# Stacking on two queues, sums and fillers on TensorE: a transformer block of self-attention, cross-attention and MLP

## The chip, the cores and the metric

The kernel runs on one NeuronCore of a Trainium2 chip. The metric is the device time of one execution in microseconds (us), the median of three runs. The engines are TensorE (PE for its matmuls, PEld for its weight loads), VectorE (DVE), ScalarE (ACT), GpSimd (POOL) and SyncE (SP, which only issues DMAs here).

## The reference

One block over x of 2 x 2048 tokens and 512 features, 16 heads of 32, with 154 context tokens per batch, in fp32:

```
xn = layer_norm(x, ln0);  q, k, v = heads(xn @ qkv_w.T)
x = x + merge(softmax(q k^T * scale) v) @ sa_proj_w.T          # self-attention
xn = layer_norm(x, ln1);  q = heads(xn @ q_w.T); k, v from the context
x = x + merge(softmax(q k^T * scale + mask) v) @ ca_proj_w.T   # cross-attention
xn = layer_norm(x, ln2)
x = x + (gelu(xn @ fc1_w.T + fc1_b) @ fc2_w.T + fc2_b)
```

## The kernel before

The program is six phases, one after the other, with a barrier of all engines between two of them: `qkv` (0 to about 311 us of the profile), `self` (to 2016), `context` (to 2066), `cross` (to 2651), `late` (to 2809) and `mlp`. Each fp32 product is split into a high and a low part (fp32r), so that three matmuls stand for one. All synchronisation is written out by hand: each engine has its own list of instructions in program order, and semaphores tie the lists. There is no scheduler. What stands behind a waiting instruction on its engine waits too.

**Self-attention** (`self_phase`) has 32 stages of 512 queries x 4 heads x 2048 keys. In a stage TensorE makes 64 first passes (scores for the row maximum, L1529, those of the stages ahead), 64 second passes (scores less maximum, L1559), and 16 times four small matmuls that weigh v with the exponentials (L1572). VectorE takes the maxima (L1697), ScalarE the exponentials (L1647). For the softmax's denominators GpSimd adds the 16 key tiles of exponentials in 8 pairs, p0 to p7 (`add_pair`, L1470), into four buffers `part_sum`, and adds one buffer onto another by accumulating DMAs of 1 MB (`add_half`, L1475): after p2, p3, p4, p5 and p6, five in a stage. At the end of block 1 of the next stage (there are 8 blocks in a stage) TensorE adds up over the partitions with ones (`add_up`, L1592) in three groups of 8 matmul instructions: one part waits for the last DMA into it, the second for p7, the third for the DMA that carries p6. Which buffer has which role changes from stage to stage (`sum_parts`), and p0 of a stage waits for the previous stage's last DMA.

**Cross-attention** (`cross_phase`) has 8 tiles of 512 tokens, 0 to 7, and 4 groups of 4 heads in each. For tile t: `project` (the output projection of self-attention, added to x, 48 matmuls), layer norm on VectorE with a power on GpSimd, `turn` (transposes), `result` (the query product, four groups of 12 matmuls into a ring `dense` of two PSUM banks, which project, turn and the maxima use too), `high_result` and `low_result` (ScalarE and VectorE split each group's result into `r_high` and `r_low`, two buffers each), `stack_q` (SP copies the parts into `q`, three places for each of four heads: 12 DMAs a group, 48 a tile), `first_pass` (L811), the maxima (`maxima`, L1100; `turn_max`; `split_max`; `send_max`, ScalarE's two DMAs into `q`), `second_pass` (L828), `exponential` (L977), `weigh_both` (L840), `add_pair` on GpSimd and `add_up` on TensorE (L850), `invert` (four reciprocals, L1117) and `divide` (L1124). `period(t)` weaves the second passes of tile t with the transposes, results and first passes of tile t+1 and the projection of tile t+2. Ahead of `period(0)` the first tile is prepared in series: project(0), norm, turn(0), the bias of the query product (L932), result(0), project(1), then the first passes of groups 0 and 1. In tile 7 nothing is left to weave in.

## Time and profile before

| | us |
|---|---|
| median of three runs | 3553.53 (3552.98 to 3554.64) |
| the profiled execution, its own time | 3546.62 |
| its span in the profile | 3544.8 |
| self-attention, 324 (first matmul) to 2016 | 1692 |
| cross-attention, 2066 to 2651 | 585 |

The profile is one execution. A windows row gives the busy time of each engine in a stretch with the number of its instructions, the mean granted clock of TensorE (1.00 is 2.4 GHz, 0.50 is 1.2 GHz) and the DMA engines' share. A timeline row gives start, length, engine, line, operation, what is written from what, shapes, how many instructions were merged, and in brackets how long the engine sat idle before and what ended it. SPq and ACTq are DMA issues.

### The profile page before, as it was taken

To read this page: it belongs to the slowest core of one execution; us is meant where nothing else is said; L and a number is where in the kernel's file an instruction comes from. 1 tells how busy PE (TensorE), PEld (TensorE's weight loads), DVE (VectorE), ACT (ScalarE), POOL (GpSimd) and SP (SyncE) were. 2 spreads that over 40 slices of the span, in tenths; PEclk is the share of its full clock that TensorE was granted. 3 is DMA by queue.
4 is the path that set the end of the run, shared out by engine and by line. 5 is a ranking of instruction groups with operands and counts; after the bars stand their busy time and mean duration, and the time that the engine had idled before them with its cause. 6 is when DMAs were issued, how large, how long until landed. Compare 5 with 4: busy or idle time off the path is not lost. (4 is left out here: it accounts for less than half of the span.)

```text
span 3544.8 us, 43782 instructions
## 1 busy us (share of the span) xinstructions
PE 3272.3 (92%) x16448; PEld 2124.6 (60%) x16448; DVE 2075.4 (59%) x3643; ACT 1541.8 (43%) x2826; POOL 1602.5 (45%) x531
## 2 busy tenths in 40 slices
PE   7998999999999999999999668898978599999999
PEld 5885555555555555555555245666536488888887
DVE  4444887778777877777787035777647532222222
ACT  2321566666666666666566413343424321111111
POOL 0001678888887888888788622343421000000000
PEclk9997899999999999999999778999959799999999
DMA  4446277677667766776675553433328721111110
GB/s 171 176 170 181 60 169 153 133 155 156 153 136 163 154 142 140 166 152 141 147 153 116 117 147 105 129 113 116 103 68 286 267 90 45 45 45 47 48 48 24
DMA packets 200516, 454.44 MB, mean 128 GB/s; under 512 B 34114, under 2 KB 57224, under 8 KB 176752
## 3 DMA queue, kind: packets, MB, share of 16 engines
q1 hardware_dynamic: 173167, 282.80, 26.0%
q0 software_dynamic: 23040, 167.78, 23.5%
q8 instruction: 130, 2.13, 0.2%
q10 hardware_dynamic: 4096, 1.06, 0.2%
q14 instruction: 83, 0.67, 0.1%
HBM read 154.47 MB, written 102.82 MB: 73 GB/s over the span
## 5 line engine op out<-in xcount | busy, mean ns | idle before, releaser
L1697 DVE TENSOR_REDUCE self_part_max<-self_first 128x1 f32<-128x512 f32 x2048 | 1250.4, 678 | 352.2 <-PE self_first L1529 352.0
L1470 POOL TENSOR_TENSOR self_part_sum<-self_expo 128x2048 f32<-128x2048 f32 x256 | 1187.5, 4647 | 274.1 <-DMA self_part_sum<-self_part_sum 209.2
L1647 ACT ACTIVATE self_expo<-self_second 128x512 f32<-128x512 f32 x2048 | 1039.3, 622 | 482.6 <-PE self_second L1559 471.5
L1529 PE MATMUL self_first<-self_k,self_q 96*128 96x512 f32 x2048 | 854.9, 425 | 13.0 <-DMA self_k<-k_t 13.0
L1559 PE MATMUL self_second<-self_q,self_k 98*128 98x512 f32 x2048 | 828.1, 406 | 14.9 <-DVE self_max_low L1709 7.0
L1529 PEld LDWEIGHTS self_first<-self_k,self_q 96*128 96x128 f32 x2048 | 397.9, 194 | 301.2 <-DVE self_part_max L1697 162.4
L1559 PEld LDWEIGHTS self_second<-self_q,self_k 98*128 98x128 f32 x2048 | 386.9, 189 | 187.0 <-ACT self_expo L1647 53.2
L1572 PE MATMUL self_weighted<-self_expo,self_v_sb 128*32 128x512 f32 x4096 | 498.3, 605 | 0.0
L2037 DVE CAST mlp_h_high<-mlp_h 128x512 fp32r<-128x512 f32 x128 | 54.8, 428 | 507.0 <-PE mlp_out_sum L61 507.0
L2012 ACT ACTIVATE mlp_h<-mlp_hidden_sum,mlp_b_col 128x512 f32<-128x512 f32 x128 | 88.3, 690 | 603.2 <-PE mlp_hidden_sum L61 603.2
L1572 PEld LDWEIGHTS self_weighted<-self_expo,self_v_sb 128*32 128x32 f32 x4096 | 107.7, 109 | 231.9 <-ACT self_expo L1647 121.0
L977 ACT ACTIVATE cross_expo<-cross_second 77x512 f32<-77x512 f32 x256 | 145.1, 592 | 216.0 <-PE cross_second L828 211.8
L726 POOL TENSOR_TENSOR cross_pair_sum<-cross_expo 77x2048 f32<-77x2048 f32 x32 | 146.2, 4569 | 178.5 <-ACT cross_expo L977 178.5
L59 PE MATMUL mlp_hidden_sum<-mlp_xt_high,mlp_w_high 128*128 128x512 f32 x512 | 203.2, 397 | 24.1 <-DMA mlp_xt_low<-xn_t 24.1
L60 PE MATMUL mlp_hidden_sum<-mlp_xt_low,mlp_w_high 128*128 128x512 f32 x512 | 202.7, 396 | 0.0
L60 PE MATMUL mlp_out_sum<-mlp_w_low,mlp_h_high 128*128 128x512 f32 x512 | 202.4, 395 | 0.0
L61 PE MATMUL mlp_out_sum<-mlp_w_high,mlp_h_low 128*128 128x512 f32 x512 | 202.2, 395 | 0.0
L61 PE MATMUL mlp_hidden_sum<-mlp_xt_high,mlp_w_low 128*128 128x512 f32 x512 | 201.9, 394 | 0.0
L59 PE MATMUL mlp_out_sum<-mlp_w_high,mlp_h_high 128*128 128x512 f32 x512 | 201.9, 394 | 0.0
L1100 DVE TENSOR_REDUCE cross_row_max<-cross_first 128x2 f32<-128x308 f32 x256 | 113.5, 454 | 87.7 <-PE cross_first L811 87.6
L1475 POOL DMA_DIRECT2D self_part_sum<-self_part_sum x160 | 141.3, 883 | 50.4 <-POOL self_part_sum L1470 37.5
L811 PEld LDWEIGHTS cross_first<-cross_k,cross_q 98*128 98x128 f32 x512 | 107.4, 224 | 50.2 <-DVE cross_row_max L1100 24.9
(162 smaller groups left out, 3848.0 us busy)
## 6 DMA issues: line engine op xcount, KB each, us to landing
self_part_sum<-self_part_sum POOLq DMA_DIRECT2D x160, 1024.0 KB, 8.3
self_k<-k_t SPq DMA_DIRECT2D x96, 256.0 KB, 9.0
self_q<-q_t SPq DMA_DIRECT2D x93, 256.0 KB, 4.7
cross_q<-cross_r_high SPq DMA_DIRECT2D x256, 64.0 KB, 2.0
qkv_x<-in_x SPq DMA_DIRECT2D x8, 1024.0 KB, 6.5
v<-qkv_v_sb SPq DMA_DIRECT2D x32, 256.0 KB, 2.1
q_t<-qkv_r_high SPq DMA_DIRECT2D x32, 256.0 KB, 2.0
q_t<-qkv_r_low SPq DMA_DIRECT2D x32, 256.0 KB, 2.3
```

What stands on the lines that cost most here:

```text
L59: nc.tensor.matmul(out, left_high, right_high, start=first, stop=False)
L60: nc.tensor.matmul(out, left_high, right_low, start=False, stop=False)
L61: return nc.tensor.matmul(out, left_low, right_high, start=False, stop=last)
L726: nc.gpsimd.tensor_tensor(pair_sum[0:width, g % pair_slots], expo[0:width, u], expo[0:width, u + 1], ALU.add).then_inc(pair_done, 1)
L977: nc.scalar.activation(expo[0:width, unit % e_slots, a], second[0:width, at % s_ring], ACT.Exp, scale=scale).then_inc(exp_done, 1)
L1470: nc.gpsimd.tensor_tensor(to, expo[:, t % p_slots], expo[:, (t + 1) % p_slots], ALU.add).then_inc(pair_done, 1)
L1475: pool.dma_start(part_sum[:, half].rearrange("p a t -> p (a t)"), part_sum[:, part].rearrange("p a t -> p (a t)"), accum_op=ALU.add).then_inc(
L1529: nc.tensor.matmul(first[:, n % f_ring], q[0:base, c % q_slots, a, s * P:(s + 1) * P], k[0:base, c // stages_per_group % 2, a, k0:k0 + TOK ...
L1559: nc.tensor.matmul(second[:, s_slot[n]], k[0:exp_rows, c // stages_per_group % 2, a, t * P:(t + 1) * P], q[0:exp_rows, c % q_slots, a], st ...
L1572: mm = nc.tensor.matmul(weighted[cols], v_sb[:, t, cols], expo[:, t % p_slots, a], start=t == 0, stop=t == n_k - 1)
L1647: nc.scalar.activation(expo[:, t % p_slots, a], second[:, s_slot[n]], ACT.Exp, scale=scale).then_inc(exp_done, 1)
L1697: nc.vector.tensor_reduce(part_max[:, a * SUB + s, k:k + 1], first[:, n % f_ring], AX_X, ALU.max).then_inc(first_read, 1)
```

## The change

Line numbers of the new kernel differ; the names are the same.

Self-attention: `add_up` has four groups instead of three. Groups 0 and 1 take the two buffers into which DMAs accumulate, groups 2 and 3 the sums p6 and p7 as GpSimd leaves them. So the DMA of p6 is gone (four a stage), the buffers keep their roles, and p0 to p3 of a stage wait for the groups 0 to 3 of the previous stage's `add_up`.

Cross-attention, start: the memset of `q` on GpSimd moves behind the first low part (`low_attn(0)`). The bias matmuls move ahead of the transposes, followed by 12 filler matmuls (`keep_busy`: a product of w_high that nobody reads). The results of groups 2 and 3 of tile 0 use the two idle `pair_sum` buffers, so that four groups have buffers of their own. ScalarE issues the DMAs of the low parts (16), SP the others (32). project(1) is woven with the first passes of group 0, and VectorE's and GpSimd's lists follow.

Cross-attention, end: fillers stand beside the first passes of group 1 of tile 7. `last_period` replaces `period(7)`: fillers, `add_last` (TensorE sums the exponentials itself, 16 matmul instructions in place of GpSimd's pair and 8), VectorE's finishing moved behind the last maxima, and a spare PSUM bank for the last sums.

```diff
+        def parts(t, g):
+            if t == 0 and g >= r_slots:
+                return r_spare[g - r_slots][:, 0], r_spare[g - r_slots][:, 1]
+            return r_high[:, g % r_slots], r_low[:, g % r_slots]
+
+        def stack(eng, t, g, places):
+            ge(eng, r_ready, groups * t + g + 1)
+            for j in places:
+                src = parts(t, g)[j % 2]
+                for a in range(heads):
+                    eng.dma_start(q[j * HEAD_DIM:(j + 1) * HEAD_DIM, heads * g + a].bitcast(F32),
+                                  src[a * HEAD_DIM:(a + 1) * HEAD_DIM].bitcast(F32)).then_inc(q_loaded[g], 16)
+
...
+                    if n < pair_slots:
+                        pool.wait_ge(q_loaded[r_slots + n], 16 * 3 * heads)
...
+                pool.wait_ge(rows_set, 1)
                 low_attn(0)
+                pool.wait_ge(a_ready, 1)
+                nc.gpsimd.memset(q[base:base + 4].bitcast(F32), 1.0).then_inc(rows_set, 1)
+                pool.wait_ge(rows_set, 2)
                 inverse_root(0)
...
+                def add_last(g):
+                    n = groups * last + g
+                    to = total if g < groups - 1 else dense[:, d_place[("maximum", last, 3)] % d_ring]
+                    if g < groups - 1:
+                        pe.wait_ge(mean_done, n)
+                    else:
+                        pe.wait_ge(max_split, n + 1)
+                    pe.wait_ge(exp_done, n_seconds * last + per_group * (g + 1))
+                    for kt in range(n_k):
+                        for a in range(heads):
+                            rows = slice(a * HEAD_DIM, (a + 1) * HEAD_DIM)
+                            mm = nc.tensor.matmul(to[rows], ones[0:width], expo[0:width, (n_k * g + kt) % e_slots, a],
+                                                  start=kt == 0, stop=kt == n_k - 1)
+                    mm.then_inc(total_done, 1)
...
+                def last_period():
+                    spare = dense_free(("maximum", last, 3))
+                    for n in range(per_group):
+                        second_pass(last, 0, n)
+                        first_pass(last, 2, n)
+                        keep_busy(spare, 1)
+                        if n == 5:
+                            add_up(last - 1, 3)
+                    for n in range(per_group):
+                        second_pass(last, 1, n)
+                        first_pass(last, 3, n)
+                        if n == 1:
+                            turn_max(last, 2)
+                        if n == 2:
+                            weigh_both(last, 0)
+                        if n == 5:
+                            add_last(0)
+                        keep_busy(spare, 1)
+                    spare = dense[:, d_place[("maximum", last, 2)] % d_ring]
+                    pe.wait_ge(max_split, groups * last + 3)
+                    for g in (2, 3):
+                        for n in range(per_group):
+                            second_pass(last, g, n)
+                            if n == 1 and g == 2:
+                                turn_max(last, 3)
+                            if n == 2:
+                                weigh_both(last, g - 1)
+                            if n == 5:
+                                add_last(g - 1)
+                            if n >= 2:
+                                keep_busy(spare, 2)
+                    weigh_both(last, 3)
+                    add_last(3)
...
+                    spare = None if has_after else dense_free(("maximum", t + 1, 1))
                     for n in range(items):
                         if has_next:
                             first_pass(t + 1, 1, n)
                         some(works[n // 4], 3)
+                        if not has_after:
+                            keep_busy(spare, 2)
...
                     rest(project(0, s))
-                for c in range(chunks):
-                    turn(0, c)
-                pe.wait_ge(w_ready, 2)
+                pe.wait_ge(w_loaded[1], 16)
                 pe.wait_ge(ln_loaded, 32)
                 for g in range(groups):
                     for c in range(chunks):
                         mm = nc.tensor.matmul(total[:, g:g + 1], w_raw[1][:, c, g * P:(g + 1) * P], shift[:, c:c + 1],
                                               start=c == 0, stop=c == chunks - 1)
                 mm.then_inc(bias_done, 1)
+                keep_busy(first[:, 0], 12)
+                for c in range(chunks):
+                    turn(0, c)
                 for g in range(groups):
                     rest(result(0, g))
-                for s in range(SUB):
-                    rest(project(1, s))
                 pe.wait_ge(ones_done, 1)
-                for g in range(2):
-                    for n in range(items):
-                        first_pass(0, g, n)
-                    turn_max(0, g)
-                for t in range(tiles):
+                for n in range(items):
+                    work = work if n % 2 else project(1, n // 2)
+                    some(work, 6)
+                    first_pass(0, 0, n)
+                    if n % 2:
+                        rest(work)
+                turn_max(0, 0)
+                for n in range(items):
+                    first_pass(0, 1, n)
+                    keep_busy(second[:, n % s_ring], 1)
+                turn_max(0, 1)
+                for t in range(last):
                     period(t)
-                add_up(tiles - 1, groups - 1)
+                last_period()
...
-                    ge(act, q_loaded[last % groups], 16 * 3 * heads * (t + 1 if last >= 0 else t))
-                    nc.scalar.activation(r_high[:, g % r_slots], dense[:, n % d_ring], ACT.Identity,
+                    if t == 1 and g < r_slots:
+                        act.wait_ge(q_loaded[g], 16 * 3 * heads)
+                    elif t > 0:
+                        before = g - r_slots
+                        act.wait_ge(q_loaded[before % groups], 16 * 3 * heads * (t + 1 if before >= 0 else t))
+                    nc.scalar.activation(parts(t, g)[0], dense[:, n % d_ring], ACT.Identity,
...
+                act.wait_ge(bias_ready, 1)
+                high_result(0, 0)
+                high_result(0, 1)
                 high_attn(1)
-                act.wait_ge(bias_ready, 1)
-                for g in range(groups):
-                    high_result(0, g)
+                high_result(0, 2)
+                stack(act, 0, 0, (1,))
+                high_result(0, 3)
+                stack(act, 0, 1, (1,))
+                stack(act, 0, 2, (1,))
+                stack(act, 0, 3, (1,))
...
+                        if n >= items - 2:
+                            invert(last - 1, 3, n - items + 2)
+                    for n in range(items):
+                        maxima(last, 3, n)
+                        if n == 0:
+                            split_max(last, 2)
+                        if n in (1, 2):
+                            invert(last - 1, 3, n + 1)
+                        if n == 2:
+                            divide(last - 1, 3)
+                    split_max(last, 3)
+                    for g in range(groups):
+                        finish(last, g)
...
+                for n in range(items):
+                    maxima(0, 0, n)
+                    if n % 2:
+                        add_projection(1, n // 2)
+                        stats_of(1, n // 2)
+                split_max(0, 0)
                 for s in range(SUB):
                     moments_of(1, s)
                 var_of(1)
-                for s in range(SUB):
-                    norm(1, s)
-                for g in range(2):
-                    for n in range(items):
-                        maxima(0, g, n)
-                    split_max(0, g)
-                for t in range(tiles):
+                for n in range(items):
+                    maxima(0, 1, n)
+                    if n >= SUB:
+                        norm(1, n - SUB)
+                split_max(0, 1)
...
-                def add_pairs(i, c):
-                    h0, h1, p0, p1 = sum_parts(c)
-                    ge(pool, half_added[0], 48 * i)
...
-                    ge(pool, total_done, n_sums * i)
-                    add_pair(i, 2, part_sum[:, p0])
-                    add_half(i, 2, 0, h0, p0)
-                    add_pair(i, 3, part_sum[:, p1])
...
+                def add_pairs(i):
+                    for p in range(4):
+                        ge(pool, total_done, n_sums * (i - 1) + p + 1)
+                        add_pair(i, p, part_sum[:, p])
+                        if p >= 2:
+                            add_half(i, p, p - 2, p)
                     if not (isinstance(i, int) and i == 0):
                         divide(i - 1)
-                    ge(pool, half_added[0], 48 * i + 16)
-                    add_pair(i, 4, part_sum[:, p0])
-                    add_half(i, 4, 0, h0, p0)
-                    ge(pool, half_added[1], 32 * i + 16)
...
+                    for p in range(4, n_pairs):
+                        half, part = p % 2, 2 + p % 2
+                        ge(pool, half_added[half], 32 * i + 16 * (p // 2 - 1))
+                        add_pair(i, p, part_sum[:, part])
+                        if p < n_pairs - 2:
+                            add_half(i, p, half, part)
...
-                    for n, part in enumerate((h1, p1, h0)):
-                        if n == 0:
-                            ge(pe, half_added[1], 32 * (i + 1))
-                        elif n == 1:
-                            ge(pe, pair_done, n_pairs * (i + 1))
+                    for n in range(n_sums):
+                        if n < 2:
+                            ge(pe, half_added[n], 32 * (i + 1))
                         else:
-                            ge(pe, half_added[0], 48 * (i + 1))
+                            ge(pe, pair_done, n_pairs * i + n_pairs - n_sums + n + 1)
```

On GpSimd in self-attention, one stage (L1470 is a pair's sum, L1475 an accumulating DMA, L1482 the division for the previous stage). Before:

```order
L1470 TENSOR_TENSOR self_part_sum<-self_expo 128x2048 x4
L1475 DMA self_part_sum<-self_part_sum 128x2048
L1470 TENSOR_TENSOR self_part_sum<-self_expo 128x2048
L1475 DMA self_part_sum<-self_part_sum 128x2048
L1482 TENSOR_TENSOR self_mean<-self_inverse,self_mean 128x512
L1470 TENSOR_TENSOR self_part_sum<-self_expo 128x2048
L1475 DMA self_part_sum<-self_part_sum 128x2048
L1470 TENSOR_TENSOR self_part_sum<-self_expo 128x2048
L1475 DMA self_part_sum<-self_part_sum 128x2048
L1470 TENSOR_TENSOR self_part_sum<-self_expo 128x2048
L1475 DMA self_part_sum<-self_part_sum 128x2048
L1470 TENSOR_TENSOR self_part_sum<-self_expo 128x2048 x4
```

The same stage now:

```order
L1575 TENSOR_TENSOR self_part_sum<-self_expo 128x2048 x5
L1580 DMA self_part_sum<-self_part_sum 128x2048
L1575 TENSOR_TENSOR self_part_sum<-self_expo 128x2048
L1580 DMA self_part_sum<-self_part_sum 128x2048
L1587 TENSOR_TENSOR self_mean<-self_inverse,self_mean 128x512
L1575 TENSOR_TENSOR self_part_sum<-self_expo 128x2048
L1580 DMA self_part_sum<-self_part_sum 128x2048
L1575 TENSOR_TENSOR self_part_sum<-self_expo 128x2048
L1580 DMA self_part_sum<-self_part_sum 128x2048
L1575 TENSOR_TENSOR self_part_sum<-self_expo 128x2048 x5
```

The DMA between p6 and p7 is gone; p6, p7 and the next stage's p0, p1, p2 follow each other directly.

On ScalarE in the first tile of cross-attention, from the transposed tile (L959) to the first maxima (L989). Before:

```order
L959 ACTIVATE cross_xt_high<-cross_dense 128x512 x4
L953 ACTIVATE cross_a_high<-cross_a_raw 128x2048
L966 ACTIVATE cross_r_high<-cross_dense,cross_q_bias 128x512 x4
L989 DMA cross_q<-cross_max_high 1x16x128
L989 DMA cross_q<-cross_max_low 1x16x128
```

And now:

```order
L1033 ACTIVATE cross_xt_high<-cross_dense 128x512 x4
L1043 ACTIVATE cross_r_high<-cross_dense,cross_q_bias 128x512 x2
L1027 ACTIVATE cross_a_high<-cross_a_raw 128x2048
L1043 ACTIVATE cross_pair_sum<-cross_dense,cross_q_bias 128x512
L637 DMA cross_q<-cross_r_low 32x512 x4
L1043 ACTIVATE cross_pair_sum<-cross_dense,cross_q_bias 128x512
L637 DMA cross_q<-cross_r_low 32x512 x4
L637 DMA cross_q<-cross_pair_sum 32x512 x8
L1067 DMA cross_q<-cross_max_high 1x16x128
L1067 DMA cross_q<-cross_max_low 1x16x128
```

Sixteen DMA issues have come onto ScalarE, and the copy of tile 1's attention (L953, now L1027) stands behind two results.

On TensorE at the end of tile 7, groups 2 and 3 (L828 second passes, L840 weighing, L850 sums). Before:

```order
L828 MATMUL cross_second<-cross_q,cross_k 77x512 x8
L840 MATMUL cross_weighted<-cross_expo,cross_v_sb 32x512 x8
L850 MATMUL cross_total<-cross_pair_sum,cross_ones 32x512 x4
L828 MATMUL cross_second<-cross_q,cross_k 77x512 x5
L840 MATMUL cross_weighted<-cross_expo,cross_v_sb 32x512 x8
L850 MATMUL cross_total<-cross_pair_sum,cross_ones 32x512 x8
```

And now, group 3 alone (L868 are fillers, L893 `add_last`):

```order
L868 MATMUL cross_dense<-cross_w_high 128x512 x2
L840 MATMUL cross_second<-cross_q,cross_k 77x512
L868 MATMUL cross_dense<-cross_w_high 128x512 x2
L840 MATMUL cross_second<-cross_q,cross_k 77x512
L893 MATMUL cross_total<-cross_expo,cross_ones 32x512 x8
L868 MATMUL cross_dense<-cross_w_high 128x512 x2
L840 MATMUL cross_second<-cross_q,cross_k 77x512
L868 MATMUL cross_dense<-cross_w_high 128x512 x2
L840 MATMUL cross_second<-cross_q,cross_k 77x512
L868 MATMUL cross_dense<-cross_w_high 128x512 x2
L852 MATMUL cross_weighted<-cross_expo,cross_v_sb 32x512 x8
L893 MATMUL cross_dense<-cross_expo,cross_ones 32x512 x8
```

The sums read the exponentials themselves, and fillers stand between the second passes.

## Rows read from the trace of the kernel before

**Rows 1.** Waits, self-attention (450 to 1950 us): who for whom, us, times, longest.
```profile
POOL self_part_sum L1470 <- DMA self_part_sum<-self_part_sum: 202.2, 106, 5.7
...
PEld self_second L1592 <- POOL self_part_sum L1470: 29.7, 17, 3.8
PEld self_second L1592 <- DMA self_part_sum<-self_part_sum: 23.7, 20, 3.1
```

**Rows 2.** Timeline, PE, line 1592: start, us, instruction, count, [idle before].
```profile
431.42 2.76 PE L1592 MATMUL self_second<-self_part_sum,self_ones 128*32 128x512 f32 x24
...
993.47 2.76 PE L1592 MATMUL self_second<-self_part_sum,self_ones 128*32 128x512 f32 x24
...
1043.47 1.90 PE L1592 MATMUL self_second<-self_part_sum,self_ones 128*32 128x512 f32 x16
...
1967.43 2.75 PE L1592 MATMUL self_second<-self_part_sum,self_ones 128*32 128x512 f32 x24
...
2009.74 1.04 PE L1592 MATMUL self_second<-self_part_sum,self_ones 128*32 128x512 f32 x8
2013.58 2.89 PE L1592 MATMUL self_second<-self_part_sum,self_ones 128*32 128x512 f32 x16 [2.80 <-POOL self_part_sum L1470]
```

**Rows 3.** Timeline, POOL: two self-attention stages, first three sums and last.
```profile
1046.07 13.68 POOL L1470 TENSOR_TENSOR self_part_sum<-self_expo 128x2048 f32<-128x2048 f32 x3 [1.87 <-DMA self_part_sum<-self_part_sum]
...
1091.10 4.56 POOL L1470 TENSOR_TENSOR self_part_sum<-self_expo 128x2048 f32<-128x2048 f32 x1 [0.71 <-DMA self_part_sum<-self_part_sum]
...
1300.97 13.69 POOL L1470 TENSOR_TENSOR self_part_sum<-self_expo 128x2048 f32<-128x2048 f32 x3 [1.17 <-DMA self_part_sum<-self_part_sum]
...
1348.66 4.51 POOL L1470 TENSOR_TENSOR self_part_sum<-self_expo 128x2048 f32<-128x2048 f32 x1 [0.27 <-DMA self_part_sum<-self_part_sum]
```

**Rows 4.** Timeline, ACT, POOL and DVE, start of cross-attention.
```profile
2074.28 1.91 ACT L953 ACTIVATE cross_a_high<-cross_a_raw 128x2048 fp32r<-128x2048 f32 x1 [22.56 <-DMA cross_a_raw<-self_t]
...
2071.20 6.92 POOL L711 MEMSET cross_q<- 4x8192 f32 x1
2078.21 6.47 POOL L716 TENSOR_TENSOR cross_a_low<-cross_a_raw,cross_a_high 128x2048 fp32r<-128x2048 f32 x1
...
2117.19 4.58 POOL L716 TENSOR_TENSOR cross_a_low<-cross_a_raw,cross_a_high 128x2048 fp32r<-128x2048 f32 x1 [15.04 <-ACT cross_a_high L953]
...
2078.02 2.29 DVE L1193 TENSOR_TENSOR cross_w_low<-cross_expo,cross_w_high 128x2048 fp32r<-128x2048 f32 x1 [11.68 <-ACT cross_w_high L1034]
```

**Rows 5.** Timeline, PE, first tile of cross-attention.
```profile
2084.78 0.76 PE L766 MATMUL cross_dense<-cross_w_high,cross_a_high 128*128 128x512 f32 x1 [22.41 <-POOL cross_a_low L716]
...
2105.12 1.97 PE L780 MATMUL cross_dense<-cross_identity,cross_a_raw 128*128 128x128 f32 x8 [6.46 <-DVE cross_a_raw L1079]
...
2109.42 6.83 PE L932 MATMUL cross_total<-cross_shift,cross_expo 128*128 128x1 f32 x32
2116.11 0.77 PE L792 MATMUL cross_dense<-cross_xt_high,cross_w_high 128*128 128x512 f32 x1
```

**Rows 6.** Timeline (SP, ACT) and windows while the first tile is stacked.
```profile
2122.97 2.44 SPq L651 DMA_DIRECT2D cross_q<-cross_r_high  x4
...
2139.57 0.69 ACT L966 ACTIVATE cross_r_high<-cross_dense,cross_q_bias 128x512 fp32r<-128x512 f32 x1 [6.90 <-DMA cross_q<-cross_r_high]
...
2122.89:2153.30 30.41, 22.04 (x82) 16.77 (x80) 8.17 (x18) 2.06 (x3) 0.00 (x0) 0.89 0.40 99
2144.85:2151.15 6.30, 6.30 (x29) 5.06 (x27) 2.77 (x4) 0.00 (x0) 0.00 (x0) 1.00 0.42 104
2151.15:2166.98 15.83, 8.64 (x35) 7.05 (x34) 11.31 (x30) 0.00 (x0) 1.01 (x1) 0.62 0.27 88
```

**Rows 7.** Window and timeline (PE, DVE), last tile of cross-attention.
```profile
2590.70:2598.70 8.00, 7.98 (x31) 6.87 (x31) 4.86 (x11) 5.31 (x10) 0.94 (x1) 0.50 0.02 4
...
2599.83 3.64 PE L840 MATMUL cross_weighted<-cross_expo,cross_v_sb 77*32 77x512 f32 x16
...
2644.20 3.40 DVE L1117 RECIPROCAL cross_total<-cross_total 128x128 f32<-128x128 f32 x4 [2.06 <-PE cross_total L850]
```

75 lines of the change are left out of this document (30 added, 45 removed).

## The prediction

> **What bounds the kernel now.** The phases run one after the other, so gains in different phases add up. I read self-attention by its waits first. GpSimd waits 202 us in 106 pieces for its own accumulating DMAs, and TensorE's weight loads wait 29.7 and 23.7 us in the sums over the partitions, for GpSimd's last pair and for the last DMA [rows 1]. TensorE is otherwise always at work, so these waits lengthen the phase. How much they cost is read from the timeline of TensorE's sums [rows 2]. Where a sum runs through in one piece (24 instructions, 2.76 us, at 993.47), the next one starts 50.00 us later. From the first (431.42) to the one at 1967.43 there are 30 periods in 1536.0 us, 36.0 more than 30 x 50.00. The last period, with no more first passes, is 42.31 us. So a stage is 50.0 us of TensorE, and 36 us are waits.
>
> In cross-attention the tiles in the middle are woven tightly; the first and the last are not. In the first, TensorE begins after 22.41 us of waiting for GpSimd's low part [rows 5], the bias (6.83 us) stands between the transposes and the results [rows 5], and then all hangs on stacking: from 2122.97 SP issues 4 DMAs in 2.44 us, 0.63 each, 48 in 30.4 us [rows 6]. ScalarE's fourth result waits 6.90 us for a buffer that such a DMA reads [rows 6], and TensorE's projection of tile 1, its ring of two banks and everything behind it wait for that result. In the last tile TensorE's granted clock is 0.50, that is 1.2 GHz. 31 matmuls, about ten pairs of second and first passes, take 8.00 us there [rows 7].
>
> **Self-attention.** A group of 8 matmul instructions adds (2.76 - 1.04) / 2 = 0.86 us, from a sum in one piece and one cut off after its first group [rows 2]. It stands on TensorE's path: 31 x 0.86 = 26.7 us more. What goes is the wait. The DMA of p6 is no longer waited for by anyone. p7 now has three groups ahead of it, 2.6 us, where it had one. And GpSimd gets ahead: it sheds a DMA issue (0.9 us between p6 and p7) and the wait ahead of its next p0, 1.87 and 1.17 us in the two stages shown [rows 3]. Its own chain from p0 to the end of p7 takes 49.6 us (1046.07 to 1095.66) and 52.2 in one of the slowest stages (1300.97 to 1353.17) [rows 3]. The new wait is that p0 needs TensorE's group 0, 0.9 us after the sum begins. With that start and 52.2 us, p7 ends at 0.9 + 52.2 - 50.86 = 2.2 us into the next sum, still ahead of its group at 2.6; with 49.6 it ends before the sum begins. So I take all 36.0 us as gone; if one wait in ten survives it is 4 us. At the phase's end one group instead of two follows p7 (1.04 of the 2.89 us [rows 2]): 1.8 less. Sum: 26.7 - 36.0 - 1.8 = **-11.1 us**, with -12 and -3 as ends.
>
> **First tile, up to the first stacked result.** The memset of q (6.92 us) leaves GpSimd's path, and the low part of tile 0 starts when ScalarE's copy ends (2076.2) instead of 2078.21 [rows 4]. It took 6.47 us where the same operation takes 4.58 at 2117.19 [rows 4]. VectorE's low weights ran from 2078.02 to 2080.31, and 2080.31 + 4.4 is when GpSimd ended: the one that came second stood still. Now GpSimd comes first, ends at 2080.8, and VectorE's 2.29 us, which the projection needs as well, end at 2083.1 rather than 2080.31. TensorE starts at 2083.1: -1.7.
>
> The Trainium skill, page "SBUF — State Buffer", says of the port pair that VectorE and GpSimd share that "issue order, not op shape, decides who blocks". By that rule the start is 2083.1; by a plain sharing of the slowdown it would be 2082.7, 0.4 us better. The rows agree with the rule.
>
> The bias now fills the wait for the normalization. It and the 12 fillers take 3.4 + 2.8 us at 2.4 GHz and 6.8 + 5.1 at 1.2; starting at 2097.0 (2084.78 + 13.9 for 48 matmuls, less 1.7) they end between 2103.2 and 2108.9, and the normalized tile is there at 2103.4 (2105.12 - 1.7) [rows 5]. I take 2104, nearer to the fast end, since TensorE comes out of 48 dense matmuls. Results follow the transposes after 4.5 us, at 2108.5 instead of 2116.11 [rows 5]: -7.6 so far. The first result's 12 matmuls run at 1.2 GHz in the profile; a warmer start gives 0 to 2.4 us, I take 1.2. The first stacking DMA goes out at 2114.2, not 2122.97: **-8.8**.
>
> **First tile, from there to the first second pass.** Before it is 2166.98 - 2122.97 = 44.0 us: stacking and project(1) to 2151.15, then 15.8 us of first passes [rows 6]. Call the first DMA's start S. With four buffers the results no longer wait for DMAs: all four groups are ready at S + 8.8. ScalarE copies tile 1's attention at S + 2.0 (it now stands behind two results, 1.9 us), GpSimd's low part (4.58 us [rows 4]) ends at S + 8.6, and project(1) starts there. Group 0 is stacked at S + 9.3 (SP's eight issues end at S + 5.1, ScalarE's four at S + 7.3, 2 us to land). Then 48 matmuls at 0.233 us (6.30 us for 27 [rows 6]) and 8 first passes at 0.37 make 14.2 us, to S + 22.8. What remains of the 15.8 us is group 1 with the statistics and normalization of tile 1 between its maxima: 8.5 us. Second passes start at S + 31.3: **-12.7 us**. All that hides is the stacking of groups 1 to 3 (SP until S + 20.2, ScalarE until S + 15.6), wanted from S + 23 on.
>
> The Trainium skill, page "DMA: Bandwidth & Descriptors", section "Issuing engines are not separate DMA queues", has two queues share the same 16 DMA engines, so that the second saves only the time of issuing. Here issuing is what takes the time: the engines' share is 0.40 while one queue issues without a pause [rows 6]. The sum changes by neither: with SP alone group 1 would be stacked by S + 17, still ahead of its use. I expect the gain from the buffers and the weave, and from the second queue next to nothing.
>
> **Last tile.** Before: 2590.70 to the end of the last division, 2644.20 + 3.40 + 0.69 = 2648.3, 57.6 us [rows 7]. Now, at 2.4 GHz: 0.9 us for the new wait on the split maximum of group 1 (its PSUM bank is the fillers'). Group 0: 8 x (second 0.23 + first 0.19 + filler 0.23) + 0.86 = 6.1. Group 1: the same 5.2, weighing 1.7 (half of 3.64 [rows 7]), `add_last` 1.7, some 1.0 for VectorE: 9.6. Groups 2 and 3: 8 second passes, 12 fillers, 1.7 + 1.7, each 8.6, and 1.0 once for a division that `add_last(1)` waits for. Then weighing and the last sum 3.4, reciprocals and division 4.1 [rows 7]. That is 42.4; with 1.4 for handoffs 43.8: **-13.8 us**. The fillers themselves are 28 x 0.23 = 6.4 us on the path, which pay only if the clock stays at 2.4 GHz. The eight pairs of fillers in tile 6 lie beside maxima that VectorE paces. The GpSimd pair that goes (4.5 us) was beside TensorE, not on the path, except at the end.
>
> **The sum.** 11.1 + 8.8 + 12.7 + 13.8 = 46.4 us. The profiled execution took 3546.6 us (span 3544.8) and would take 3500.2. The median of the runs is 3553.5, 6.9 more than the profiled one; I see no row for that and carry it over: 3553.5 - 46.4 = **3507**.
>
> **Rivals.** (1) *GpSimd's chain paces self-attention after all.* For: GpSimd waits 202 us for DMAs that stay [rows 1], and p0 is now tied to TensorE's sum. Against: 49.6 us against 50.86. If half of the waits stay, 18 us are lost: 3525. (2) *The clock stays at 1.2 GHz in the last tile.* For: it is so now, and has not risen although TensorE was busy 7.98 of 8.00 us [rows 7]. Against: the tile before leaves TensorE busier than it was when the clock fell, and the fillers are matmuls like those from 2144.85 on, whose clock is 1.00 [rows 6]. Then the 40.2 us of TensorE and waits before the last 3.4 + 4.1 grow by about 27 in all, the tile takes 71 us, and the kernel 3534. (3) *Something in the first tile takes the place of the buffer wait*, the normalization of tile 1 or the copy on ScalarE behind the results: half of the 21.5 us comes, 3518. (4) *Slower than before:* the loop from group 0 to p0 to p7 becomes the stage's length. Each stage has four DMAs in series with eight sums; if they landed so much later that the chain took over 50.86 + 46.4 / 31 = 52.4 us in every stage, the rest's gain would be eaten. At 53.0 it is 31 x 2.1 = 66 us more in self-attention: 3573. The slow stage shown, 52.2, is close, but few stages come near it, and there is a DMA less. (5) *The change does not do what it says*: the fillers or the queue turn out inert; that lies within the range.
>
> **How the numbers follow.** Forecast 0.68 (3499 to 3516); rival 1 0.09, rival 2 0.09, rival 3 0.10, rival 4 0.03, and 0.01 for a result within 0.2% of before, about what a measurement of this kernel can tell from no change. The range of 8 in 10 takes in rivals 1 and 3 in part and stops short of 2: 3497 to 3527. Faster by over 0.2%: 0.96; within: 0.01; slower: 0.03.
>
> **What would show it.** In the profile of the changed kernel the sums of self-attention should stand 50.9 us apart throughout, 32 instructions in one piece, with no wait for GpSimd or a DMA. In cross-attention TensorE should start about 17 us after the barrier, the second passes of tile 0 about 21 us earlier than before from the phase's start, and the last tile should have a granted clock of 1.00 and take 44 us. The prediction is wrong if self-attention's sums still wait, if that clock is 0.50, or if TensorE waits more than 2 us for a normalization in the first tile.

## The result, and the profile after

The changed kernel takes 3499.84 us (median; 3498.54 to 3504.63), the kernel before 3553.53: 53.7 us less. The ratio, 0.9863 with an interval of 0.9845 to 0.988, gives a little less than the medians: 49 us (43 to 55). The forecast was 3507, 46.4 us less. The profiled execution of the changed kernel is its slowest, 3504.63 us (span 3502.8), 42.0 us shorter than the profiled one of before.

By phase, between the barriers, in the two profiled executions and in a second one of the kernel before that an experiment below gave:

| us | before | before, second profile | after |
|---|---|---|---|
| start of the program to cross-attention's barrier | 2066.2 | 2073.4 | 2058.6 |
| cross-attention: barrier to the first second pass | 100.8 | 100.8 | 77.3 |
| tiles 0 to 6, to the first second pass of tile 7 | 423.7 | 423.4 | 424.1 |
| tile 7, to the end of the last division | 57.6 | 57.9 | 44.2 |
| what follows, to the end of the span | 896.5 | 898.2 | 898.7 |

**Self-attention.** The timeline of TensorE's sums, which stands against [rows 2]: in the stages shown a sum is one piece of 32 instructions with no wait in front. In 30 of the 32 stages it takes 3.6 us so; the other two sums take 3.85 and 4.01.

```profile
430.84 3.62 PE L1682 MATMUL self_second<-self_part_sum,self_ones 128*32 128x512 f32 x32
...
991.20 3.62 PE L1682 MATMUL self_second<-self_part_sum,self_ones 128*32 128x512 f32 x32
...
1042.06 3.62 PE L1682 MATMUL self_second<-self_part_sum,self_ones 128*32 128x512 f32 x32
...
2006.40 3.65 PE L1682 MATMUL self_second<-self_part_sum,self_ones 128*32 128x512 f32 x32
```

The waits of the same phase (who for whom, us, times, longest), against [rows 1]:

```profile
POOL self_part_sum L1575 <- DMA self_part_sum<-self_part_sum: 190.1, 91, 5.9
...
POOL self_part_sum L1575 <- PE self_second L1682: 43.2, 23, 4.7
...
PEld self_second L1682 <- POOL self_part_sum L1575: 3.2, 7, 1.1
```

GpSimd still waits for its DMAs, 190 us instead of 202, and has a new wait of 43 us for TensorE's sums; but TensorE's weight loads wait 3.2 us where they waited 29.7 + 23.7. GpSimd's timeline, against [rows 3], shows the two ends of that loop: p7 ends at 1037.22 + 4.59 = 1041.81, just ahead of the sums (1042.06), and p0 starts 1.2 us behind their first instruction; from there to the next p7's end (1093.62) it is 50.4 us.

```profile
1037.22 4.59 POOL L1575 TENSOR_TENSOR self_part_sum<-self_expo 128x2048 f32<-128x2048 f32 x1 [1.51 <-DMA self_part_sum<-self_part_sum]
1043.22 13.70 POOL L1575 TENSOR_TENSOR self_part_sum<-self_expo 128x2048 f32<-128x2048 f32 x3 [1.40 <-PE self_second L1682]
...
1089.04 4.58 POOL L1575 TENSOR_TENSOR self_part_sum<-self_expo 128x2048 f32<-128x2048 f32 x1 [1.55 <-DMA self_part_sum<-self_part_sum]
```

**First tile.** The barrier is at 2058.56 here and was at 2066.18. Timeline of GpSimd, VectorE, TensorE and SP, against [rows 4] and [rows 5]:

```profile
2069.02 4.50 POOL L722 TENSOR_TENSOR cross_a_low<-cross_a_raw,cross_a_high 128x2048 fp32r<-128x2048 f32 x1 [5.50 <-ACT cross_a_high L1027]
...
2070.70 4.97 DVE L1299 TENSOR_TENSOR cross_w_low<-cross_expo,cross_w_high 128x2048 fp32r<-128x2048 f32 x1 [11.98 <-ACT cross_w_high L1112]
...
2075.82 0.77 PE L778 MATMUL cross_dense<-cross_w_high,cross_a_high 128*128 128x512 f32 x1 [21.08 <-DVE cross_w_low L1299]
...
2088.76 3.63 PE L998 MATMUL cross_total<-cross_shift,cross_expo 128*128 128x1 f32 x32
2092.26 4.60 PE L868 MATMUL cross_first<-cross_w_high 128*128 128x512 f32 x12
2096.69 1.03 PE L792 MATMUL cross_dense<-cross_identity,cross_a_raw 128*128 128x128 f32 x8
...
2105.44 10.24 SPq L637 DMA_DIRECT2D cross_q<-cross_r_high  x16
```

The bias takes 3.63 us and not 6.83. TensorE's first second pass is at 2135.89. The window from the first stacking DMA to it (busy time of PE, PEld, DVE, ACT, POOL with counts, clock, DMA share, GB/s), against [rows 6]:

```profile
2105.44:2135.89 30.45, 26.55 (x120) 21.27 (x119) 16.82 (x39) 3.87 (x4) 5.60 (x2) 0.91 0.58 163
```

**Last tile.** Windows, against [rows 7] (the second is a stretch of an ordinary tile, for later), and the last reciprocals and division:

```profile
2564.00:2598.70 34.70, 34.02 (x214) 15.96 (x216) 22.05 (x36) 17.58 (x32) 0.00 (x0) 1.00 0.07 25
...
2257.00:2263.80 6.80, 5.95 (x25) 5.58 (x26) 4.49 (x10) 3.37 (x7) 0.00 (x0) 0.50 0.04 12
...
2600.01 3.40 DVE L1206 RECIPROCAL cross_dense<-cross_dense 128x128 f32<-128x128 f32 x4 [1.51 <-PE cross_dense L893]
2603.45 0.69 DVE L1213 TENSOR_TENSOR cross_mean<-cross_dense,cross_mean 128x512 f32<-128x512 f32 x1
```

The clock is 1.00 as long as TensorE works on the tile, where it was 0.50.

### The profile page after: what moved, and what is told of

Read it like the earlier page. It is cut to its first block and busy times, and to the rows that moved or that the text cites. A ratio compares the mean times of both kernels' runs of the same rounds, so it can differ in the third digit from the quotient of the medians.

```text
span 3502.8 us, 44500 instructions
## 1 busy us (share of the span) xinstructions
PE 3281.3 (94%) x16812; PEld 2133.4 (61%) x16812; DVE 2078.2 (59%) x3643; ACT 1541.9 (44%) x2826; POOL 1553.9 (44%) x495
## 5 line engine op out<-in xcount | busy, mean ns | idle before, releaser
L734 POOL TENSOR_TENSOR cross_pair_sum<-cross_expo 77x2048 f32<-77x2048 f32 x28 | 128.1, 4574 | 133.9 <-ACT cross_expo L1055 133.9
L1580 POOL DMA_DIRECT2D self_part_sum<-self_part_sum x128 | 112.9, 882 | 41.0 <-POOL self_part_sum L1575 33.1
```

Source lines behind the costliest of these rows:

```text
L734: nc.gpsimd.tensor_tensor(pair_sum[0:width, g % pair_slots], expo[0:width, u], expo[0:width, u + 1], ALU.add).then_inc(pair_done, 1)
```

## The experiments

All ratios are to the kernel before on the same chip. The times of one kernel scatter by 9 to 25 us on the chips of the experiments, more than in the first measurement. The changed kernel itself was timed only in the first measurement, so an experiment is held against it by the two ratios, which are good to some 6 to 8 us each. Where a single stretch is in question, the profile decides it; each kernel has one.

### One part at a time

Three kernels hold one part each; a fourth is the kernel before, unchanged, with a second profile.

```diff
# x1_self: only (cut)
-    n_sums = 3
+    n_sums = 4
# with the loops on GpSimd and TensorE that follow from it
```

> The kernel before with the change of self-attention alone (four groups of sums, the DMA of p6 gone). Theory A, the prediction's: eight more matmul instructions a stage cost 26.7 us and all 36.0 us of waits go, so the whole is about 11 us faster than before (between 3 and 12). Theory B: the profile of the changed kernel shows only 7.6 us gained ahead of cross-attention, since one stage took 54.2 us and the clock was low at the phase's end; if that is the rule and not one execution's accident, the gain is 7 to 8 us. Theory C: GpSimd's chain or the DMAs still pace some stages in most executions, gain under 4 us. If the parts add up, this one is also what is left of 53.7 us when the first tile (about 23) and the last (about 13) are taken off: 17 us, and then the profiled execution of before flatters before.

Measured: 3541.84 us, ratio 0.9976 (0.9962 to 0.9989), 8.5 us less by the ratio (4 to 13). In its profile the barrier of cross-attention stands at 2058.8, 14.6 us ahead of the second profile of before. Its cross-attention, which is that of before, is 5.1 us longer than in that profile (590.5 us against 585.4): two tiles took 64.9 us, where that profile has one and the first none, and tile 6 took 60.8 instead of 57.5. So in the phase itself the gain is above theory A's, theory C falls, and the time alone would have misled.

`x2_first` has only what changed at the start of cross-attention, as in the diff of the change: the memset behind the low part, the bias and 12 fillers ahead of the transposes, four buffers, `stack` on SP and ScalarE, the weave with 8 fillers.

> The kernel before with the changes at the start of cross-attention alone (memset behind the low part, bias ahead of the transposes with 12 fillers, four result buffers, two stacking queues, project(1) woven with first passes). Theory A: the parts are independent, and it gains what the two profiles show between the barrier and the first second pass, 100.8 - 77.3 = 23.5 us (the prediction had 21.5). Theory B: a later phase gives some of it back (the granted clock of the tiles behind it, or the period in which the second passes start at 1.2 GHz), gain 15 to 20 us.

Measured: 3526.64 us, ratio 0.9928 (0.9905 to 0.995), 26 us less (18 to 34). In the profile 77.2 us from the barrier to the first second pass, and cross-attention 560.3 us, 25.1 less. Theory A.

```diff
# x3_last: only (cut; add_last, the fillers and VectorE's new order come with it)
-    for t in range(tiles): period(t)
+    for t in range(last): period(t)
+    last_period()
```

> The kernel before with the changes at the end of cross-attention alone (fillers in tile 6 and 7, sums on TensorE, the finishing behind the last maxima). Theory A: 13 to 14 us faster, last tile 44 us at a granted clock of 1.00 throughout. Theory B: whether the clock holds hangs on how the tile before was met, and in a kernel with another start it falls in some executions: then 3 to 8 us, with a clock of 0.50 for part of the tile and times that scatter.

Measured: 3538.69 us, ratio 0.9968 (0.9951 to 0.9984), 11 us less (6 to 17). Last tile 44.2 us in the profile. Theory A. The three sum up to 8.5 + 25.6 + 11.4 = 45.5 us by their ratios and to 15 + 25 + 12 = 52 us by their profiles; the whole change is 49 us by its ratio and 54 by the medians. Within that scatter the parts add up.

> The kernel before once more, unchanged, for its profile beside its times. The prediction carried over 6.9 us between the profiled execution (3546.6) and the median (3553.5) with no row for it. Theory A: it is chance of one execution or another chip, and a second profile shows a time within 2 us of the median, with more waiting in self-attention than the 36 us read from the first one. Theory B: profiled executions are always shorter than timed ones by about 7 us; then this profile is again near 3546.

Measured: 3555.38 us, ratio 1.0003 (0.9985 to 1.0021), profiled span 3553.7 us. Theory A: profiled executions are not short as such. The timeline of its sums, start, length, instruction, count and wait:

```profile
431.19 2.76 PE L1592 MATMUL self_second<-self_part_sum,self_ones 128*32 128x512 f32 x24
...
2016.99 1.04 PE L1592 MATMUL self_second<-self_part_sum,self_ones 128*32 128x512 f32 x8
...
2020.79 2.92 PE L1592 MATMUL self_second<-self_part_sum,self_ones 128*32 128x512 f32 x16 [2.75 <-POOL self_part_sum L1470]
```

The last sum starts 1585.8 us behind the first, and 1578.3 in [rows 2]. The kernels x2 and x3, whose self-attention is that of before, have 1586.6 and 1585.8. An execution with 1578.3 is the odd one of four: beyond 30 periods of 50.00 us and a last one of 42.3 it has 36 us, which are the waits, the others 43.5 to 44.3. (It is also the only one of the four from the first measurement; whether the execution or the chip makes the difference is open.)

### The cushion of three groups

```diff
# y5_p7_first: the groups in the order p7, buffer 0, buffer 1, p6
-                    for n in range(n_sums):
+                    for at in range(n_sums):
+                        n = (at - 1) % n_sums
# and GpSimd's waits for the groups in the same order
-                        ge(pool, total_done, n_sums * (i - 1) + p + 1)
+                        ge(pool, total_done, n_sums * (i - 1) + (p + 1) % n_sums + 1)
```

> The changed kernel with the four groups of sums in self-attention in another order: p7 first, then the two buffers of the DMAs, then p6 (GpSimd's waits follow the same order). It tests the cushion: in the changed kernel p7 is read last, 2.6 us behind the start of the sums, and in its profiles GpSimd ends p7 between 7 us before the start and 3.5 us behind it. Theory A: those 2.6 us are what swallows the waits. Read first, p7 is late in 20 of the 31 stages by 0.2 to 3.5 us, some 26 us in all by the changed kernel's profile, less what GpSimd gains back from waiting less; the phase is 15 to 30 us longer and most of the gain over the kernel before is gone. Theory B: the missing DMA of p6 is what helped, and the order does not matter: under 5 us.

Measured: 3545.32 us, ratio 0.9976 (0.9961 to 0.9991). The barrier of cross-attention is at 2109.0 instead of 2058.6, 50 us later. But the profiled execution is this kernel's slowest, 3558.51 us, 13 above the median; by the two ratios the order costs some 40 us. Either way it is theory A's mechanism, above the 30 us that I gave it. Its sums and GpSimd's timeline:

```profile
1011.50 3.62 PE L1683 MATMUL self_second<-self_part_sum,self_ones 128*32 128x512 f32 x32
...
1062.98 3.64 PE L1683 MATMUL self_second<-self_part_sum,self_ones 128*32 128x512 f32 x32 [0.44 <-POOL self_part_sum L1575]
...
1013.51 13.69 POOL L1575 TENSOR_TENSOR self_part_sum<-self_expo 128x2048 f32<-128x2048 f32 x3 [3.00 <-PE self_second L1683]
...
1058.26 4.58 POOL L1575 TENSOR_TENSOR self_part_sum<-self_expo 128x2048 f32<-128x2048 f32 x1 [1.25 <-DMA self_part_sum<-self_part_sum]
1065.01 13.68 POOL L1575 TENSOR_TENSOR self_part_sum<-self_expo 128x2048 f32<-128x2048 f32 x3 [2.17 <-PE self_second L1683]
```

Now a loop closes: the sums wait for p7, GpSimd's next p0 waits 2.2 to 3.0 us for the first groups of the sums, and from p0 to the end of p7 it needs 49.3 us (1013.51 to 1062.84). The stage is what the loop takes, 51.5 us here and 52.3 on average ((2054.70 - 432.67) / 31), where TensorE has 50.9 of work. I had priced the delays one by one, as if GpSimd could recover; in a loop each is paid for by the next stage too. In the changed kernel the same loop is 50.4 + 1.2 us (the rows above) less the 2.6 of the groups ahead of p7, 49.0 against 50.9. With p7 first the whole gain in self-attention is lost, and more. What the missing DMA of p6 brings by itself was not tried.

### The first tile: queue, buffers, weave

```diff
# y1_one_queue
-                    stack(sp, t, g, (0, 1, 2) if t > 0 else (0, 2))
+                    stack(sp, t, g, (0, 1, 2))
-                stack(act, 0, 0, (1,))        # and those of groups 1 to 3
```

> The changed kernel with all 48 stacking DMAs of the first tile on SP, none on ScalarE. Theory A, the prediction's: the second queue is worth next to nothing. Group 0 is stacked after SP's twelve issues (7.6 us) instead of eight, about 2 us later, ahead of the projection's first part, whose GpSimd copy it waits for anyway; the first second pass starts within 1 us of 77.3 us behind the barrier, and the time is that of the changed kernel within 1 us. Theory B: issuing bounds the first tile, so the groups come 7.6 us apart and the second passes of tile 0 start 5 us or more later.

Measured: 3501.8 us, ratio 0.9865 (0.9849 to 0.9882); first second pass 77.2 us behind the barrier. Theory A.

```diff
# y3_two_buffers
-            if t == 0 and g >= r_slots:
-                return r_spare[g - r_slots][:, 0], r_spare[g - r_slots][:, 1]
# ScalarE stacks groups 0 and 1 ahead of results 2 and 3, which wait for them
```

> The changed kernel with two result buffers in the first tile as before (groups 2 and 3 wait until groups 0 and 1 are stacked), and all else changed: two queues, the weave, bias and fillers. Theory A: the buffers are a large part of the 12.7 us (13.5 measured) between the first stacking DMA and the first second pass. Group 2's result then waits for group 0's stacking, about 9 us behind the first DMA, group 3's for group 1's, about 14 us, and the projection of tile 1 with them: second passes 4 to 8 us later. Theory B: the weave hides the buffers' wait, as the maxima and the normalization of tile 1 set the end: under 2 us.

Measured: 3505.44 us, ratio 0.9878 (0.9859 to 0.9897); first second pass 78.3 us behind the barrier. Theory B, by the profile. (The profiled execution takes 3512.86 us, its slowest; two of its tiles take 66.2 and 65.7 us, where the changed kernel has one of 65.0.)

```diff
# y8_two_buf_one_q: both of these
```

> The changed kernel with two result buffers and one stacking queue in the first tile, as before; weave, bias, fillers and the rest as changed. One queue alone cost nothing (first second pass 77.2 us behind the barrier), two buffers alone 1.0 us (78.3). Theory A: either one hides the lack of the other, and both together cost more than the sum: the third result waits for twelve issues and a landing (9.6 us behind the first DMA), the fourth for twelve more (17.2), the projection's second part for that, and second passes start 4 to 7 us later. Theory B: the weave hides both, under 2 us.

Measured: 84.5 us to the first second pass, 7.2 later than in the changed kernel: a little over theory A's range. ScalarE's timeline shows the wait of [rows 6] back, for two results:

```profile
2114.94 0.69 ACT L1039 ACTIVATE cross_r_high<-cross_dense,cross_q_bias 128x512 fp32r<-128x512 f32 x1 [5.29 <-DMA cross_q<-cross_r_high]
...
2122.51 0.69 ACT L1039 ACTIVATE cross_r_high<-cross_dense,cross_q_bias 128x512 fp32r<-128x512 f32 x1 [6.89 <-DMA cross_q<-cross_r_high]
```

Its time, 3506.09 us (ratio 0.9869, 0.9852 to 0.9886), is not to be told from the changed kernel's. Tiles 0 to 2 are shorter in its profile (54.2, 60.6 and 60.1 us against 55.6, 60.9 and 61.1 in y1, with one queue and four buffers), so that of 7.3 us 3.4 are left at tile 7. The windows over tile 0, y8 and then y1, show what differs:

```profile
2143.57:2197.80 54.23, 51.92 (x301) 34.45 (x302) 36.84 (x70) 25.54 (x45) 22.82 (x5) 1.00 0.40 113
...
2131.67:2187.30 55.63, 53.92 (x301) 36.31 (x302) 36.97 (x70) 25.73 (x45) 22.82 (x5) 0.96 0.45 132
```

The matmuls are the same, the granted clock is 1.00 instead of 0.96, and in tiles 1 and 2 it is 0.97 instead of 0.94. So a part of what the first tile loses comes back through the clock; why the clock falls less there is open, and it is one profile each.

```diff
# y7_no_weave
-                for n in range(items):
-                    work = work if n % 2 else project(1, n // 2)
-                    some(work, 6)
-                    first_pass(0, 0, n)
+                for s in range(SUB):
+                    rest(project(1, s))
+                for n in range(items):
+                    first_pass(0, 0, n)
# and VectorE's order of before
```

> The changed kernel with the projection of tile 1 in one piece ahead of the first passes of tile 0, and VectorE's statistics and normalization ahead of its maxima, as in the kernel before; four buffers and both queues stay. From the first stacking DMA to the first second pass it was 44.0 us before and is 30.5 now. Theory A: the weave is worth about 5 us of that: the projection starts 8.6 us behind the first DMA, takes 11.2 for 48 matmuls, and 15.8 us of first passes follow, 35.6. Theory B: since the two-buffer kernel is only 1 us later at this point, all 13.5 us hang on the weave, and the stretch is 42 to 44 us.

Measured: 3510.05 us, ratio 0.9878 (0.986 to 0.9896); first second pass 84.1 us behind the barrier. From the first stacking DMA it is 37.2 us, near theory A's 35.6. So the stretch from the first stacking DMA to the first second pass, by what a kernel has in its first tile (the one without the weave and with two buffers is the kernel before, which lacks the bias's new place and the fillers too):

| buffers | queues | weave | us |
|---|---|---|---|
| 2 | 1 | no | 44.0 (before, both profiles) |
| 2 | 1 | yes | 37.6 |
| 2 | 2 | yes | 31.6 |
| 4 | 1 | yes | 30.5 |
| 4 | 2 | no | 37.2 |
| 4 | 2 | yes | 30.5 |

Half of the 13.5 us is the weave (6.8), half is that groups 2 and 3 need not wait for stacking (6.8 for buffers and queue together without the weave). For the second half, with the weave, either the buffers or the queue will do: given the one, the other is worth 0.1 us (queue) and 1.2 (buffers); without it, 6.0 (queue) and 7.1 (buffers). Issuing sets the pace of stacking (0.63 us a DMA on one queue), and that is what the second queue relieves. The Trainium skill, page "DMA: Bandwidth & Descriptors", section "Issuing engines are not separate DMA queues", says that a second issuing engine saves this time alone, and that it is usually small beside the transfer. Here it is 0.63 us beside some 2 us from issue to landing, but 48 DMAs stand in one row, and with two buffers the second queue brings 6.0 us.

### The fillers

```diff
# y2_no_fill_last
-                        keep_busy(spare, 1)      # and all others in last_period and period(6)
```

> The changed kernel without the fillers beside group 1 of tile 7 and without those in tile 7 (TensorE still sums the exponentials itself). Theory A: the fillers hold the clock. Without them the granted clock falls to 0.50 in the last tile as in the kernel before, the tile takes 50 to 58 us instead of 44.2, and the kernel is 6 to 13 us slower than the changed one. Theory B: the gain is from the summing on TensorE and the order of VectorE's work; then the tile takes 38 to 44 us, since 28 fillers of 0.23 us leave the path (6.4 us).

Measured: 3514.65 us, ratio 0.9899 (0.9883 to 0.9916). The last tile takes 59.2 us (second pass at 2557.59, last division ends at 2616.76), 15.0 more than with fillers and 1.6 more than before the change. The window over most of it:

```profile
2560.00:2600.00 40.00, 39.02 (x143) 14.72 (x142) 19.42 (x33) 15.62 (x28) 0.00 (x0) 0.50 0.06 23
```

Theory A, a little beyond its upper end. What is left of the change in this tile is by itself a loss of 1.6 us. The summing on TensorE adds 4 x (3.64 - 1.94) = 6.8 us (16 matmuls of the new sum and 8 of the old one, both in y2's profile) to an engine that is busy 39.0 of 40.0 us. Against that, a wait of the kernel before is gone, that of its last sum for VectorE's division:

```profile
2642.20 1.93 PE L850 MATMUL cross_total<-cross_pair_sum,cross_ones 77*32 77x512 f32 x8 [4.25 <-DVE cross_mean L1124]
```

No run has the fillers without the summing, or VectorE's new order alone, so y2 shows what the fillers are worth beside the other two, and not what each of those is worth.

The same holds for the middle of cross-attention. In each of tiles 1 to 6 of the changed kernel TensorE waits for the normalized next tile, and the granted clock is 0.50 for 6.8 us behind that (the window 2257.00 to 2263.80 above):

```profile
2257.85 1.11 PE L792 MATMUL cross_dense<-cross_identity,cross_a_raw 128*128 128x128 f32 x4 [4.17 <-DVE cross_a_raw L1163]
```

```diff
# z1_fill_tiles, in period(t), after the second pair of passes
+                        if n == 1 and has_next and t > 0:
+                            pe.wait_ge(exp_done, n_seconds * t + 1)
+                            keep_busy(second[:, (n_seconds * t + 2) % s_ring], 14)
```

> The changed kernel with 14 more fillers in each of tiles 1 to 6, behind the second pair of passes, where TensorE waits 4.2 us for the normalized next tile. In the trace of the changed kernel each such wait is followed by 6.8 us at a granted clock of 0.50. Theory A: the fillers fit into the wait (14 x 0.233 = 3.3 us), the clock stays at 1.00, and each tile is up to 3.4 us shorter, 58 instead of 61.3: up to 20 us faster than the changed kernel. Theory B: what ends the period is not TensorE in those 6.8 us but ScalarE's or VectorE's chain, which runs no faster; then the clock is 1.00 and the period the same within 0.5 us. Theory C: the fillers push the transposes later and cost 1 us a tile.

Measured: 3482.54 us, ratio 0.9815 (0.9798 to 0.9832), 17 us less than the changed kernel by the two ratios. Its timeline and window in the place where the clock was low:

```profile
2247.12 3.50 PE L868 MATMUL cross_second<-cross_w_high 128*128 128x512 f32 x14 [0.16 <-ACT cross_expo L1058]
...
2251.12 0.65 PE L792 MATMUL cross_dense<-cross_identity,cross_a_raw 128*128 128x128 f32 x4 [0.50 <-DVE cross_a_raw L1166]
...
2251.12:2258.00 6.88, 6.59 (x43) 5.20 (x43) 6.24 (x14) 6.13 (x13) 1.65 (x1) 1.00 0.12 19
```

The 14 fillers fit the wait, the clock is 1.00 behind them and in all of tiles 0 to 7, and tiles 1 to 5 take 58.8 to 59.2 us instead of 61.1 to 65.0. Cross-attention is 528.7 us, not 549.3. Theory A below its upper price: 2.0 to 2.7 us a tile come back, of 3.4. Besides, there is no tile of 65 us, which six of the twelve profiles without these fillers have once or twice. 1.6 of the 20.6 us lie ahead of tile 0's second passes (75.7 us instead of 77.3) and 1.5 in tile 0 (54.1 instead of 55.6), where this kernel has none of the new fillers. The granted clock differs there: in the changed kernel it is 0.57 from 2093 to 2097, where the first tile's 12 fillers take 4.60 us, and 0.67 from 2128 to 2136; in z1 it is 1.00 in both places, and the 12 take 2.97. Why the clock holds in z1 ahead of its first new filler is open.

```diff
# z2_fill_starts: z1, and ahead of the first matmul of two phases
+                for _ in range(66):
+                    nc.tensor.transpose(first[:, 0, 0:P], identity[:], identity[:])
```

> The kernel with fillers in tiles 1 to 6 (3482.5 us) and, besides, transposes of the identity that nobody reads while TensorE waits for its first operands: 66 at the start of cross-attention and 56 at the start of the phase behind it. In the changed kernel the first matmuls of these phases run at a granted clock of 0.50, for 3.7 and 6.1 us. Theory A: the clock is then 1.00 from the first matmul on and 1.9 and 3.0 us are gained, 5 us in all. Theory B: small transposes do not raise the clock, or the gain disappears in waits behind it (the next operands are not there sooner): no change within 1 us. Theory C: the transposes last longer than the wait and push the first matmul back by 1 to 4 us.

Measured: 3484.73 us, ratio 0.9806 (0.9787 to 0.9826), and 75.7 us from the barrier to the first second pass, as in z1. No gain over z1 that can be told, as theory B has it, but not for either of its reasons: the granted clock did rise to 1.00 while the transposes ran (0.77 on average over them), but they were over 6.7 us ahead of the first matmul, which found it at 0.50 again. At the start of the next phase the same happened with 5.3 us.

```profile
2057.11 9.56 PE L998 MATMUL cross_first<-cross_identity 128*128 128x128 f32 x66 [4.52 <-POOL cross_minus_half L718]
...
2073.33 0.77 PE L780 MATMUL cross_dense<-cross_w_high,cross_a_high 128*128 128x512 f32 x1 [6.66 <-DVE cross_w_low L1306]
```

The 12 + 8 fillers of the change's own first tile were not tried alone. In the changed kernel the transposes behind the 12 start at 2096.69, while VectorE has the normalized tile ready at 2095.34: the 12, half of them at 1.2 GHz, hold TensorE up by some 1.3 us.

## Where the prediction was right, and where not

**Self-attention, -11.1: right in every step but the size of the waits.** Eight more instructions cost 3.62 - 2.76 = 0.86 us, the period is 50.86 to 51.0 as forecast, p7 is at worst 3.3 us into the sums, the last groups swallow it, and 3 us of waits survive. (The 3.3 us are the latest p7 of nine profiles with four groups, the last stage left out, where it comes up to 7.5 us into the sums.) But the 36.0 us of waits were those of one execution; three others have 43.5 to 44.3. The gain to the barrier is 13.6 us if the mean of nine profiles with four groups (2058.0) is held against the mean of four with three (2071.6).

**The step that failed** is in the sum: "6.9 more than the profiled one; I see no row for that and carry it over". Those 6.9 us are, by x4, 7.5 us of self-attention's waits, the very thing that the change removes. It is read from x4, whose time is its kernel's median and whose cross-attention is as long as in the first profile; the timed executions of the first measurement have no profile. They should have gone with the waits; 3546.6 - 46.4 = 3500.2 was the better forecast, for a reason that the prediction didn't have. Between the two profiled executions the change brought 42.0 us, less than the 46.4 of the sum. The 53.7 of the medians are these 42.0, the 6.9, and 4.8 by which the profiled execution of the changed kernel is above its median.

**First tile up to the first stacking DMA, -8.8: measured -9.9** (46.9 us from the barrier instead of 56.8). TensorE starts 17.3 us behind the barrier (forecast 16.9). VectorE's low weights took 4.97 us, 2.82 until GpSimd had ended and 2.15 more: the one that came second stood still, as the prediction read it and as the Trainium skill, page "SBUF — State Buffer", section "Who interferes with whom", has it ("Issue order, not op shape, decides who blocks"). The first result starts at +42.2 (forecast 42.3). The last term, the results at a higher clock, gave 2.2 us (6.9 to 4.7 from the first result to the first DMA) where I took 1.2.

**From there to the first second pass, -12.7: measured -13.5**, 30.45 us against 31.3. The attribution was half right. "Next to nothing" for the second queue holds, but only beside four buffers; it would have saved 6.0 us without them. And the weave is worth as much as the buffers.

**Last tile, -13.8: measured -13.4**, 44.2 us against 43.8, with the clock at 1.00. The sum has two slips. Tile 7 has 40 fillers (8, 8, 12 and 12 in the four groups), not 28; the groups' terms have all 40, but "28 x 0.23 = 6.4 us on the path" should be 9.2. And 8 second passes, 12 fillers, 1.7 and 1.7 make 8.0, not 8.6; groups 2 and 3 took 9.5 and 9.6 us, so that both 8.6 and the 1.4 for handoffs were needed, and the total is near by some luck. Rival 2 was priced at 71 us for a tile whose clock stays low. Without fillers, at 1.2 GHz, it took 59.2; 40 fillers 0.43 us apart would make it some 76, an estimate. That the fillers pay only through the clock is what the prediction said, and y2 shows it.

**The rivals.** (1) and (4), GpSimd's chain, did not happen, but y5 shows that the loop of (4) is real and near: 1.9 us a stage away. (2) did not happen. (3) neither: TensorE waited 1.7 us ahead of the projection of tile 1, for GpSimd's low part, which was in the sum, and 0.7 and 1.4 us at the first tile's maxima. The profiled execution of the changed kernel lost 3.3 us in one stage of 54.2, where TensorE waited 1.5 us for the row maxima's DMA and the granted clock was 0.97, and 3.6 in one tile of 65.0; its other executions are 4 to 6 us faster.

## What to carry to other kernels

Before a profile's waits are counted, look how far that one execution stands from the median: what it lacks is likely in the waits, and belongs to the term that removes them. The same holds the other way: y5's profiled execution is 13 us above its median, and its profile overstates what the order costs. In a loop of two engines, what counts is the work that the waited-for item has ahead of it in the consumer: moving p7 from the last place to the first cost 40 to 50 us with the same instructions. And where TensorE waits a few us for another engine in a loop, fill the wait: here what followed ran at half the clock, in six tiles. The fillers have to reach up to the next real matmul; those of z2 ended 6.7 us ahead of it and brought nothing.

## What the runs showed of the hardware

- Around a wait of 4.2 us and the matmuls behind it TensorE's granted clock was 0.50 for 6.8 us, in each of six tiles; with 14 matmuls that nobody reads in that wait it was 1.00, and the kernel 17 us shorter. Where TensorE was busy 39.0 of 40.0 us without fillers, the clock stayed at 0.50 all the same (y2).
- In half of the profiles a second stretch at 0.50 stands in tile 2, in two of them in tile 4 too, at 3.5 us or more each; in some one stands in tile 6. They are part of the scatter, and hid 5 of the 14.6 us in x1. No long wait stands ahead of it: in the changed kernel TensorE was busy 6.17 of the 7.00 us before (windows below). Why the clock falls there, in some executions and not in others, is open.

```profile
2284.00:2291.00 7.00, 6.17 (x32) 3.92 (x34) 2.80 (x6) 5.42 (x8) 3.74 (x1) 1.00 0.49 133
2291.10:2297.90 6.80, 6.80 (x30) 3.15 (x23) 1.35 (x2) 0.59 (x1) 5.20 (x2) 0.50 0.49 134
```

- A transpose of 128 x 128 took 9.56 / 66 = 0.145 us on average, and the granted clock rose from 0.50 to 1.00 while a row of 66 ran.
- Executions of the same self-attention differ by up to 8 us (1578.3 to 1586.6), in the waits of TensorE's sums for GpSimd and its DMAs.
